# A scan, windowed attention and routed FFN in one program: a store count of its own, an earlier row gather, later weight loads

## What is computed

```python
u = einsum('bct,bcd->bdt', x, weights[conditions])        # a weight per sequence
x = x + selective_scan(u, softplus(...), A, B, C, D)      # 512 channels, 16 states, 64 steps
q, k, v = project(x)                                      # rms norm and rope on q and k
k_blocks = k_blocks.at[blk, :, off, :].set(k)             # paged keys and values, 257 blocks a sequence
v_blocks = v_blocks.at[blk, :, off, :].set(v)
p = softmax(where(in_window_of_256, q @ k_all, -inf))
a = (p @ v_all) @ Wo
_, idx = top_k(a @ w_r + b_r, l // 2)                     # the router keeps half the tokens of a sequence
h = gelu(a[idx] @ w1 + b1)
x = x + zeros_like(a).at[idx].set(h @ w2 + b2)
```

## Time and profile before

| | us |
|---|---|
| median of three runs | 1921.63 (1917.76, 1921.63, 1927.96) |
| the profiled execution | 1918.95 |
| its span, from the first to the last instruction | 1917.2 |

### The profile page before, as it was taken

One profiled execution on the slowest core, in us unless ns is written; L12 is line 12 of the kernel. 1 busy time (PEld: TensorE's weight loads), 2 busy tenths in 40 slices (PEclk: granted clock), 3 DMA queues, 4 the chain that ended last, 5 costly groups with the idle time before them and its releaser, 6 DMA issues. The chain is left out here.

```text
span 1917.2 us, 30895 instructions
## 1 busy us (share of the span) xinstructions
PE 1671.0 (87%) x9719; PEld 1166.0 (61%) x9719; DVE 1458.0 (76%) x2572; ACT 1281.8 (67%) x4024; POOL 1232.6 (64%) x1127
## 2 busy tenths in 40 slices
PE   6778888888888888866777699999999999999998
PEld 5665666666556666644345475756657575665765
DVE  8997999999999999999577465655656565665522
ACT  6775888888888888877366474655646465564621
POOL 5777899999999999988677745444444544440000
PEclk9988999999999999999888799999999999999999
DMA  6433343344434443341477534434343343431011
GB/s 222 157 125 109 146 162 126 133 167 162 137 125 165 162 147 125 138 160 50 130 222 228 162 89 115 121 109 123 94 142 100 108 120 108 124 95 60 30 61 46
DMA packets 141273, 244.63 MB, mean 128 GB/s; under 512 B 32488, under 2 KB 95996, under 8 KB 135736
## 3 DMA queue, kind: packets, MB, share of 16 engines
q1 hardware_dynamic: 108024, 177.38, 26.9%
q0 software_dynamic: 33088, 65.28, 12.4%
HBM read 221.79 MB, written 48.89 MB: 141 GB/s over the span
## 5 line engine op out<-in xcount | busy, mean ns | idle before, releaser
L1082 DVE TENSOR_TENSOR_SCAN hid<-scan_psum,hid 128x1024 f32<-128x1024 f32 x256 | 581.3, 2271 | 22.4 <-ACT scan_psum L692 22.4
L1286 PE MATMUL scan_psum<-ident,hid 128*128 128x128 f32 x2048 | 341.1, 286 | 115.7 <-POOL hid L533 113.6
L1286 PEld LDWEIGHTS scan_psum<-ident,hid 128*128 128x128 f32 x2048 | 254.5, 146 | 273.7 <-POOL hid L533 145.5
L1542 POOL DMA_INDIRECT kv_at<-in_kv_rows,idx_old x183 | 178.8, 977 | 299.5 <-PE attn_psum L1939 257.6
L533 POOL TENSOR_TENSOR hid<-hid,kv_at 128x1024 f32<-128x1024 f32 x128 | 307.0, 2411 | 41.1 <-DVE hid L1082 40.4
L533 POOL TENSOR_TENSOR hid<-hid,bc 128x1024 f32<-128x1024 f32 x128 | 306.2, 2405 | 28.7 <-DVE hid L1082 28.2
L1762 DVE CUSTOM_DVE_ANT_0 prob<-attn_psum,mask 128x336 f32<-128x336 f32 x256 | 119.7, 505 | 240.9 <-PE attn_psum L1919 240.7
L1624 ACT COPY p_t<-attn_psum 112x384 f32<-112x384 f32 x256 | 122.6, 485 | 247.4 <-PE attn_psum L1926 247.4
L2009 PE MATMUL attn_psum<-w,ffn_hid 128*128 128x512 f32 x512 | 238.5, 595 | 4.9 <-DVE y_sb L1826 4.9
L1993 PE MATMUL attn_psum<-xs_in,w 128*128 128x256 f32 x1024 | 233.4, 382 | 6.7 <-ACT xs_in L1630 5.8
L1550 POOL DMA_INDIRECT kv_at<-kv_scratch,idx_new x189 | 196.3, 1038 | 62.0 <-issue 56.4
(11 more groups left out here) (224 smaller groups left out, 3024.1 us busy)
## 6 DMA issues: line engine op xcount, KB each, us to landing
bc<-bc_scratch SPq DMA_DIRECT2D x16, 2048.0 KB, 9.7
kv_at<-bc_scratch SPq DMA_DIRECT2D x15, 2048.0 KB, 9.9
q_scratch<-qg SPq DMA_DIRECT2D x32, 260.0 KB, 2.0
early<-q_scratch SPq DMA_DIRECT2D x32, 260.0 KB, 3.2
x_pair<-in_x_pairs SPq DMA_DIRECT2D x32, 256.0 KB, 4.3
f_wo<-in_w_o SPq DMA_DIRECT2D x32, 256.0 KB, 3.3
kv_scratch<-kvg SPq DMA_DIRECT2D x32, 256.0 KB, 2.0
a_scratch<-a_sb SPq DMA_DIRECT2D x32, 256.0 KB, 2.8
```

What stands on the lines that cost most here:

```text
L1082: nc.vector.tensor_tensor_scan(states, decay[k % 2], states, 0.0, ALU.mult, ALU.add).then_inc(dve_h, 1)
L1286: mm = nc.tensor.matmul(yc[g], hid[:, e % RING, i, P * g:P * g + P], ident[:], start=False, stop=(k % 4 == 3 and i == 3), is_transpose=Tru ...
L1542: pool.indirect_dma_start(kv[s][:, c, :], None, A["kv_rows"], bass.IndirectOffsetOnAxis(ap=idx_old[:, c, b:b + 1], axis=0)).then_inc(ld_ol ...
```

## The change

Three edits.

First, the stores of `r_out` count on a semaphore of their own, `st_r`. `take_product(n)` now waits for `n` stores of `f_out`, `take_route(n)` for `n - 1` stores of `r_out`, and the end of the block for both. To have a semaphore free, two others are merged: `c_neg` counts on `c_a`, whose waits go up by one, and `dve_lt` on `c_dve` (in `last_groups` `then` becomes `link`, which does the same on `c_dve`).

Second, in `eight(i)` the call `gather(i, s)` comes after the gathers of kept rows.

Third, the four parts of the second weights are loaded in pairs 4 to 7 instead of 3 to 6.

```diff
@@ store_products
-                    sp.dma_start(S["w_or"][:, P * (s % NCH):P * (s % NCH) + P], r_out[0:1, :]).then_inc(st_w, 16)
+                    sp.dma_start(S["w_or"][:, P * (s % NCH):P * (s % NCH) + P], r_out[0:1, :]).then_inc(st_r, 16)
...
@@ end of SP's part of the scan block
-            sp.wait_ge(st_w, 16 * folds(4 * NT))
+            sp.wait_ge(st_w, 16 * 4 * NT)
+            sp.wait_ge(st_r, 16 * NROUTE)
...
@@ take_product, take_route
                     act.wait_ge(pe_fold, folds(n) + 1)
-                    wait(act, st_w, 16 * folds(n))
+                    wait(act, st_w, 16 * n)
                     nc.scalar.copy(f_out[:], y[0][:, SUB:2 * SUB]).then_inc(act_fold, 1)
...
                     act.wait_ge(pe_fold, folds(n))
-                    wait(act, st_w, 16 * (folds(n - 1) + 1))
+                    wait(act, st_r, 16 * (n - 1))
                     nc.scalar.copy(r_out[0:1, :], y[1][0:1, SUB:SUB + P]).then_inc(act_fold, 1)
...
@@ merged counts (four waits on c_a go up by one, like this one; every then in last_groups becomes link)
-            nc.scalar.activation(neg_a[:], a_log, ACT.Exp).then_inc(c_neg, 1)
+            nc.scalar.activation(neg_a[:], a_log, ACT.Exp).then_inc(c_a, 1)
...
-                dve.wait_ge(c_neg, 1)
+                dve.wait_ge(c_a, 1)
...
-                    then(v.tensor_tensor(last_sq[n], raw, raw, ALU.mult))
+                    link(v.tensor_tensor(last_sq[n], raw, raw, ALU.mult))
...
@@ SP, pair
-                if isinstance(m, int) and 1 <= m < NCH + 3:
-
-                    n, c = NF // NCH, m - 3
+                if isinstance(m, int) and 1 <= m < 2 * NCH:
+
+                    n, c = NF // NCH, m - NCH
...
@@ POOL, eight
                 for s in range(NKV):
-                    gather(i, s)
                     if s == 5:
                         gather_rows(i - 1, 0)
                     if s == 1 and not (isinstance(i, int) and i == 1):
                         gather_rows(i - 2, 1)
+                    gather(i, s)
```

More of the change, by code:

```diff
@@ L212, in scan_block @@
         at_ok, ld_found, ld_first = sem("at_ok"), sem("ld_found"), sem("ld_first")
-        c_a, c_neg, c_dve, c_sin = sem("c_a"), sem("c_neg"), sem("c_dve"), sem("c_sin")
+        c_a, c_dve, c_sin = sem("c_a"), sem("c_dve"), sem("c_sin")
         wnow_ok, wpair_ok = sem("wnow_ok"), sem("wpair_ok")
@@ L235, in scan_block @@
         pe_turn, act_x1 = sem("pe_turn"), sem("act_x1")
-        ld_wo, ld_fw, pe_fold, act_fold, st_w = sem("ld_wo"), sem("ld_fw"), sem("pe_fold"), sem("act_fold"), sem("st_w")
+        ld_wo, ld_fw, pe_fold, act_fold = sem("ld_wo"), sem("ld_fw"), sem("pe_fold"), sem("act_fold")
+        st_w, st_r = sem("st_w"), sem("st_r")
         pe_last, act_lc, act_lr = sem("pe_last"), sem("act_lc"), sem("act_lr")
-        dve_lt, dve_ls, dve_lk = sem("dve_lt"), sem("dve_ls"), sem("dve_lk")
+        dve_ls, dve_lk = sem("dve_ls"), sem("dve_lk")
         C_AT = 11
@@ L385, in quarter @@
                 if isinstance(t, int) and t == 0 and q == 2:
-                    sp.wait_ge(c_a, 4)
+                    sp.wait_ge(c_a, 5)
                     sp.dma_start(S["cos"], cos[:]).then_inc(st_rope, 16)
@@ L551, in quarter @@
                         if isinstance(t, int) and s == 3:
-                            pool.wait_ge(c_a, 4)
+                            pool.wait_ge(c_a, 5)
                             pool.wait_ge(zero_ok, N_ZERO)
@@ L663, in sines @@
                 nc.scalar.activation(sin[:], rem, ACT.Sin).then_inc(c_a, 1)
-                act.wait_ge(c_a, 1)
+                act.wait_ge(c_a, 2)
                 nc.scalar.activation(cos[:], rem, ACT.Sin, scale=0.5).then_inc(c_a, 1)
             def cosines(last):
-                act.wait_ge(c_a, 3 if last else 2)
+                act.wait_ge(c_a, 4 if last else 3)
                 if last:
@@ L1025, in last_groups @@
             def last_groups():
[L1027 to L1032, removed]
                 for n, (g, i) in enumerate(LAST):
@@ L1054, in last_groups @@
                         continue
-                    then(v.scalar_tensor_tensor(rs, r3, 1.5, r0, ALU.add, ALU.mult))
+                    link(v.scalar_tensor_tensor(rs, r3, 1.5, r0, ALU.add, ALU.mult))
                     k_in, k_on, k_by, k_to = (x.rearrange("p (g d) -> p g d", g=G) for x in
                                               (raw, last_kn[n], last_rot[n], kvg[p][:, 0:G * HD]))
-                    then(v.tensor_tensor(k_on, k_in, rs.unsqueeze(2).to_broadcast([P, G, HD]), ALU.mult))
+                    link(v.tensor_tensor(k_on, k_in, rs.unsqueeze(2).to_broadcast([P, G, HD]), ALU.mult))
                     for j in range(2):
@@ L1063, in last_groups @@
                                                  .to_broadcast([P, G, HALF]), ALU.mult)
[L1064 to L1065 removed]
+                    link(k_half)
+                    link(v.tensor_tensor(k_in, k_on, last_cos[n].unsqueeze(1).to_broadcast([P, G, HD]), ALU.mult))
                     v.tensor_tensor(k_to, k_in, k_by, ALU.add).then_inc(dve_lk, 1)
```

6 lines of the change are left out of this document (3 added, 3 removed).

## The result

The changed kernel takes 1893.63 us (median, 1891.99 to 1898.64), the kernel before 1923.22 us in the runs beside it: a ratio of 0.9851, 95% interval 0.9818 to 0.9884. It is about 29 us faster (28.7 by the ratio, 29.6 by the medians); 1899 was forecast, with a range of 1888 to 1910.

The account below looks back on a forecast made before the run. DVE was taken to bound the scan and PE the second half. From 1918.95 us, 12.6, 8.2 and 0.6 came off, giving 1897.6; half of a 2.7 us offset was added for a forecast of 1899, range 1888 to 1910.

Parts of the forecast that it names:

- The bound and the places: DVE bounds the scan, PE the second half; gains come only from idle DVE in the scan or PE at attention's start.
- Both named waits: ACT's four waits before `f_out` for the store of `r_out` go; PE's first `x_rows` wait, 8.94 us, falls nearly away.
- One sign: In the scan, DVE's four large waits for ACT between 80 and 200 us fall to under 1 us each.
- Part 1: In the scan, `f_out` no longer waits for the store of `r_out`: 12.6 us gained, bounds 7.8 and 15.98.
- DVE gains the smaller of its own wait and ACT's: Step for the scan, taken at each of four waits: 1.26 + 2.24 + 5.59 + 3.52 = 12.61 us.
- Part 2: At attention's start, `x_rows` passes six gathers on POOL; PE's second wait stays but ends earlier: 8.2 us gained.
- The first rival: At attention's start, gathers don't really occupy POOL or another wait replaces `x_rows`: no gain there, 1906.3 us, chance 0.08.
- The other 14 moves: Later in attention, PE doesn't wait for `x_rows` again; POOL may stand for the index, but three pairs cover it: 0.
- Part 3: Second weights a pair later remove POOL's 1.26 us landing wait in pair 3: 0.6 us gained, 0 to 1.26.
- That the scan gives nothing: Rival: in the scan, PE becomes the late one once the stores aren't; 1910.2 us, chance 0.07.
- that the start of attention gives nothing: Rival: POOL's gathers don't really occupy it, or another wait ends where `x_rows` did; 1906.3 us, chance 0.08.
- The slower case: Rival: in attention, `x_rows` heading POOL's queue holds six gathers for 10 us at nine tiles; 1987 us, chance 0.03.

Follow-up runs that it names:

- e7: Changed kernel with PE's router product one step earlier in quarters 1 to 4 (step 2 instead of 3): 1887.72 us, ratio 0.9818.
- e1: Kernel before with only the separate count for stores of `r_out` and the merged counts: 1902.58 us, ratio 0.9892.
- e10: Changed kernel with chained copies added on ACT before `f_out` in quarters 2 to 5, as long as the old store waits: 1910.74 us, ratio 0.9957.
- e4: The changed kernel run again, unaltered, beside the kernel before: 1892.83 us, ratio 0.9847.
- e5: Changed kernel with kept rows gathered ahead of only three of a sequence's six gathers: 1899.38 us, ratio 0.9879.
- e6: Changed kernel with both gathers of kept rows two steps of `eight` sooner, passing twelve more gathers: 1883.28 us, ratio 0.9802.
- e8: Changed kernel with the second weights loaded in pairs 3 to 6 again: 1894.74 us, ratio 0.9864.
- e2: Kernel before with only the new order in `eight`, kept rows gathered ahead of a sequence's rows: 1912.49 us, ratio 0.9948.
- e3: Kernel before with only the second weights loaded a pair later: 1919.06 us, ratio 0.9989.

## Why the prediction was right, and where its sum was not

**The bound and the places: right.** DVE is the scan's bound and PE the second half's, before and after. Both named waits did what was said: none of `f_out` ends with a store, and PE's first `x_rows` wait is gone. One sign did not come: DVE's waits for ACT between 80 and 200 us were to fall under 1 us each, and 1.41, 2.65 and 1.08 us are left, at 86, 139 and 169 us; the 2.65 stands behind `r_out`, which e7 then took away.

**Part 1: right mechanism, too small a term.** The sum took 12.6 us, at most 15.98; e1 measured 18.3 (interval of the ratio: 17.1 to 24.4), e10 put 17.9 back. The traces give about the same: DVE opens quarter 7 at 227.9 us in the mean of six traces with the new counts (the changed kernel, e1, e4, e5, e6, e8) and at 244.5 in the mean of three with the old (the kernel before, e2, e3), 16.6 us apart. The step that failed is "DVE gains the smaller of its own wait and ACT's". It took one wait from each quarter, that of the scan behind `f_out`, and left the others as they were. For quarter 4 that was 5.59; the quarter shrank by 37.10 - 29.37 = 7.73. Two other scans of that quarter, in the kernel before:

```profile
150.82 2.29 DVE L1082 TENSOR_TENSOR_SCAN hid<-scan_psum,hid 128x1024 f32<-128x1024 f32 x1 [1.34 <-ACT scan_psum L692]
...
175.31 2.29 DVE L1082 TENSOR_TENSOR_SCAN hid<-scan_psum,hid 128x1024 f32<-128x1024 f32 x1 [2.08 <-ACT scan_psum L692]
```

and after:

```profile
150.58 2.29 DVE L1077 TENSOR_TENSOR_SCAN hid<-scan_psum,hid 128x1024 f32<-128x1024 f32 x1 [0.48 <-ACT scan_psum L694]
...
168.57 2.29 DVE L1077 TENSOR_TENSOR_SCAN hid<-scan_psum,hid 128x1024 f32<-128x1024 f32 x1 [1.08 <-ACT scan_psum L694]
```

These two fell by 0.86 and 1.00 us with the big one. Quarter 5 is alike: 33.33 - 28.14 = 5.19 us where the sum had 3.52. In the two quarters 12.9 us came where 9.1 were forecast, and that is most of the miss. The rest of the 16.6 lies before quarter 4, where the sum had 3.5 and the traces differ by 3.4 in the mean (DVE opens quarter 4 at 143.3 and 146.7 us). That part is the least sure: between the two profiled executions themselves quarter 4 opens 1.0 us later after the change (144.00 and 144.99), so that the scan gains 11.9 us there and the program 20.3, close to the forecast 12.6 and 21.4. This agreement is luck: too much forecast for the early quarters against too little for quarters 4 and 5.

What stands behind the smaller waits is PE. Both are scans for which ACT had first to take something from PE: for the first `qg` from the projection, for the second `drg` (`take_x`) and `r_out`. ACT's wait for `r_out` is 2.11 us in both kernels; the one for `drg` went from 2.09 to 0.44. The stretch from 145 to 185 us by engines, with the granted clock third from the end, in the kernel before, after, and in e10:

```profile
145.00:185.00 40.00, 32.51 (x153) 23.08 (x152) 30.46 (x19) 23.43 (x83) 28.61 (x29) 0.78 0.30 111
```

```profile
145.00:185.00 40.00, 35.10 (x195) 24.91 (x194) 37.25 (x25) 30.65 (x108) 35.96 (x36) 0.96 0.40 135
```

```profile
145.00:185.00 40.00, 32.62 (x152) 23.02 (x151) 30.47 (x20) 28.53 (x96) 28.82 (x26) 0.77 0.30 111
```

With ACT standing, PE does 153 matmuls there instead of 195, at a granted clock of 0.78 instead of 0.96: of the 40 slices of 1 us in this stretch, 15 have a granted clock of 0.50 in the kernel before and 16 in e10, and 2 after the change. The ten microseconds from 160 us on hold nine of the 15 slices; in the kernel before `drg` comes at their end (169.95). Again before, after and in e10:

```profile
160.00:170.00 10.00, 8.33 (x35) 6.86 (x36) 10.00 (x7) 7.91 (x30) 6.97 (x5) 0.52 0.41 174
```

```profile
160.00:170.00 10.00, 6.27 (x52) 5.71 (x52) 8.91 (x6) 7.45 (x29) 8.89 (x5) 1.00 0.51 204
```

```profile
160.00:170.00 10.00, 7.70 (x32) 6.52 (x33) 9.48 (x6) 8.48 (x31) 6.36 (x5) 0.51 0.48 200
```

In the five microseconds before that, with ACT standing, PE was busy for 2.55 us in the kernel before and 3.29 in e10, after the change for 4.51. Two matmuls of the projection for `qg`, about 144 us, in the kernel before, after, and in e10:

```profile
143.87 1.92 PE L1195 MATMUL scan_psum<-w_qkv,early 128*128 128x512 f32 x2
```

```profile
144.57 1.02 PE L1190 MATMUL scan_psum<-w_qkv,early 128*128 128x512 f32 x2
```

```profile
144.57 1.91 PE L1197 MATMUL scan_psum<-w_qkv,early 128*128 128x512 f32 x2
```

The pair takes 0.9 us longer in the kernel before and in e10, where the granted clock over its 1.92 and 1.91 us is 0.50; over its 1.02 us after the change it is 1.00. And `qg` on ACT comes 4.03 us after the quarter's opening before (4.07 in e10) and 2.80 after. So here the stall of ACT costs DVE 5.67 us directly, and then 0.86 and 1.00 us more behind a PE that is late, at a granted clock of 0.50 over the pair of matmuls and of 0.52 from 160 to 170 us. That e10 brings the clock and the late projection back without any store shows that ACT's standing is the cause; that the clock rather than PE's later start makes the smaller waits is shown by the 0.9 us of this pair and, in quarter 3, by two traces with the same scan, the kernel before and e2, in the view of stretches:

```profile
113.00:119.00 6.00, 6.00 (x30) 4.05 (x30) 6.00 (x6) 3.07 (x10) 5.94 (x3) 1.00 0.01 3
```

```profile
113.00:119.00 6.00, 6.00 (x23) 3.68 (x22) 5.55 (x5) 1.32 (x6) 5.92 (x3) 0.76 0.00 0
```

PE is busy throughout in both, but does 30 matmuls at a granted clock of 1.00 and 23 at 0.76; ACT then waits 1.74 and 4.64 us for `qg`. The store's wait is alike (3.10 and 2.84 us), and the quarter takes 30.27 and 34.36 us. Why the clock was lower in e2 there isn't shown, and for the other smaller waits the clock's part is argued. In the three rows of the stretch the lower clock goes with fewer matmuls (0.78, 0.96 and 0.77, with 153, 195 and 152); which of the two comes first isn't shown by them.

**Part 2: right, 8.2 forecast, 8.4 measured** (e2; 6.7 to 13.2 by the interval; 7.6 to 8.8 by POOL's issue of the second `x_rows`). PE's second wait stayed and POOL stayed its limit, as worked out from POOL's rows. The first rival, that the gathers don't really occupy POOL, doesn't fit: passing six of them is worth 8.4 us, passing twelve more another 9 until the index is late (e6), and POOL's row shows some 1.3 us for each (7.84 and 8.18 for six). The other 14 moves show no cost in PE's waits, as said, though POOL's wait for the index went from 129.3 to 284.3 us.

**Part 3: right place, time not told.** 0.6 was forecast, at most 1.26; e3 has 1.9 with an interval that takes in nothing. In e3's one trace POOL issues the second `x_rows` 2.4 to 3.0 us sooner after its first gather than in the kernel before and e1, so the one visible wait was probably too small a measure. The wait that it was to remove is gone, and its cover holds: the last load is issued at 1093.48, no landing of these loads is over 10.5 us, and the first reader at 1125.16 doesn't wait.

**The rivals.** That the scan gives nothing fell with e1 and that the start of attention gives nothing with e2, each by its part alone. The slower case fell by the changed kernel's waits and by e6. The forecast of 1899 was 5.4 us too long. The gain itself was missed by more: 21.4 forecast, 28.1 (e4) to 29.6 measured, of which the term of the scan is about 4 to 6 and part 3 may be one more. That the time came nearer is luck of the base: the forecast counts from 1920.3 (the profiled execution and half of 2.7), and the kernel before took 1923.22 in the runs beside the changed one.

**What stays open.** The traces give the scan 16.6 us and the runs of e1 18.3; traces with the same scan differ by up to 4 us at the same place (DVE's quarter 7 opens between 225.6 and 229.7 us with the new counts), so I can't say whether the remaining 2 us are real. In e1 PE's first wait for `x_rows` was only 2.40 us and its second 13.17, with the order of before; its two landings took 4.9 and 3.4 us instead of 8.4 and 5.9. Why they were shorter wasn't tested. The landing of the second `x_rows` varies without regard to the parts, from 3.3 us (e3) to 7.0 (the changed kernel), while e4, the same kernel, has 3.3: a wait of PE's that ends with it can't be read to better than that from one trace.

## What to carry to other kernels

When an engine stands behind a wait, count every later wait of the bound engine in that stage that hangs on the standing engine or on PE, not only the next one: here it was 16 to 18 us instead of 12.6. One count for two stores makes the copy to one buffer wait for the store of the other (3.10 to 5.59 us, four times, here); give each buffer its own. In a queue of gathers that are issued one by one (about 1.3 us each here), the one with the nearest use goes first, until its index is what it waits for; and a wait that is left after such a move (here 11.5 us for the second rows, 7.4 us for the router's product) is the next thing to take: both together brought another 20 us.

## What the runs showed of the hardware

- With ACT standing for 16 us spread over four quarters, for a store or for added copies, PE's granted clock in the 40 us around the longest of these stalls was 0.78 and 0.77 instead of 0.96, and quarters 4 and 5 of the scan took 12.9 and 12.8 us longer for 9.1 us of standing.
- With PE busy for 6.00 of 6.00 us, the same scan had 30 matmuls done at a granted clock of 1.00 and 23 at 0.76; the quarter took 30.27 and 34.36 us.
- An indirect gather on POOL costs its queue about 1.3 us (six in 7.84 and 8.18 us); moving one ahead of six others was worth 8.4 us, and ahead of twelve more another 9.
- 1 MB weight loads issued beside a run of gathers go with a POOL wait of 1.26 to 2.80 us for a landing in the four traces where the first of them lay in pair 3; with the loads a pair later that wait is gone in all eight.
